# One range of 80 nodes per block, the edge attributes in the products, and gathers that no longer wait for the segment sums

## The reference

```python
f0 = x0 @ W1_0e / sqrt(32);  f1 = einsum('nui,uw->nwi', x1, W1_1o) / sqrt(32)
feat0, self0, feat1, self1 = halves of f0 and f1          # 32 units each
e0 = feat0[src];  e1 = feat1[src]                          # gather, 128 numbers per edge
ea0 = edge_attr_4[:, :1];  ea1 = edge_attr_4[:, 1:4]
h = gelu(gelu(edge_attr_8 @ W_mlp1 / sqrt(8)) @ W_mlp2 / 8)
w00, w01, w10, w11 = h @ Wp_..                             # 32 weights each, per edge
out0_a = w00 * e0 * ea0;              out0_b = w11 * sum(e1 * ea1) / sqrt(3)
out1_a = (w01 * e0) * ea1;            out1_b = w10 * e1 * ea0
n0, n1 = segment_sum of [out0_a, out0_b], [out1_a, out1_b] over dst
y = cos * self + sin * (n @ W2)                            # W2_0e, W2_1o
out = layernorm(x + y)
```

## Time and profile before

| | |
|---|---|
| median of the runs | 5078.59 us |
| the profiled execution | 5022.96 us, its span 5021.2 us |
| share of the span busy | PE 73%, PE weight loads 52%, DVE 37%, ACT 27%, POOL 63% |
| granted TensorE clock, mean | 0.861 |
| gathers | 3224 indirect DMAs, 211.52 MB, 16.2% of the 16 DMA engines |
| moved by DMA, mean | 51 GB/s |

### The profile page before, as it was taken

The page is one execution under the profiler, slowest core; times in us unless marked ns, Lnnn a source line. Parts: engine busy times, 40 slices in busy tenths (PEclk is TensorE's granted clock), DMA queues, the critical chain, the costliest instruction groups (busy, mean ns, idle before and its releaser), DMA issues.

```text
span 5021.2 us, 43952 instructions
## 1 busy us (share of the span) xinstructions
PE 3679.1 (73%) x13222; PEld 2590.0 (52%) x13222; DVE 1875.9 (37%) x4551; ACT 1335.7 (27%) x2651; POOL 3166.7 (63%) x3262
## 2 busy tenths in 40 slices
PE   7667777767777777767777777777777677777776
PEld 4445555545555555444555545554555455555555
DVE  4333333333333333333333334333433343334335
ACT  4222222222222222222222222222222222222224
POOL 5656666666666666666666666666666666666660
PEclk8888888888888888888888888898888888888887
DMA  4111111211111121111112111111111111111111
GB/s 162 48 43 48 50 46 48 50 47 47 49 49 48 46 50 48 47 47 46 45 47 50 48 46 50 48 48 49 47 48 50 46 48 50 48 47 47 48 45 57
DMA packets 244371, 254.65 MB, mean 51 GB/s; under 512 B 162332, under 2 KB 188703, under 8 KB 242800
## 3 DMA queue, kind: packets, MB, share of 16 engines
q0 software_dynamic: 103616, 211.52, 16.2%
q1 hardware_dynamic: 139024, 42.54, 3.4%
q10 hardware_dynamic: 1696, 0.18, 0.0%
HBM read 241.18 MB, written 12.80 MB: 51 GB/s over the span
## 4 chain that ended last, share of the span: by engine, by line
another core or an unknown queue 56%; PE 29%; ACT 8%; issue 6%; DVE 1%; ACTq 0%; DMA 0%; DVEq 0%; POOL 0%; POOLq 0%
PE bank L778 9%; PE bank L769 8%; PE bank L764 6%; ACT h L551 3%; PE bank L790 2%; PE bank L798 1%; ACT big L557 1%; ACT idx L536 1%; ACT ztsb L570 1%; ACT dst_rows L566 1%; ACT big L622 1%; ACT dst_rows L565 1%; ACT dst_rows L564 1%; PE bank L723 0%
## 5 line engine op out<-in xcount | busy, mean ns | idle before, releaser
L456 POOL DMA_INDIRECT gath<-feature_table,idx x3224 | 3144.5, 975 | 1733.1 <-issue 1598.8
L769 PE MATMUL bank<-h,w2bd 128*128 128x512 f32 x800 | 580.3, 816 | 1207.2 <-ACT h L551 1150.3
L1042 DVE TENSOR_TENSOR big<-bank,gath 128x256 f32<-128x256 f32 x606 | 254.3, 420 | 2947.8 <-remote 2807.5
L551 ACT ACTIVATE h<-bank 128x512 f32<-128x512 f32 x400 | 238.9, 597 | 3305.3 <-remote 2832.0
L790 PE MATMUL bank<-big,sel 128*128 128x256 f32 x4848 | 1081.3, 379 | 7.3 <-DVE big L1045 7.3
L778 PEld LDWEIGHTS bank<-wpbd,big 128*128 128x128 f32 x3224 | 742.4, 230 | 525.8 <-issue 358.3
L790 PEld LDWEIGHTS bank<-big,sel 128*128 128x128 f32 x4848 | 922.5, 190 | 133.3 <-issue 7.5
L778 PE MATMUL bank<-wpbd,big 128*128 128x256 f32 x3224 | 969.5, 441 | 1.2 <-DVE big L1045 1.2
L769 PEld LDWEIGHTS bank<-h,w2bd 128*128 128x128 f32 x800 | 151.6, 237 | 1379.9 <-ACT h L551 1316.7
L1045 DVE TENSOR_TENSOR big<-bank,gath 128x384 f32<-128x384 f32 x1212 | 613.5, 548 | 0.0
L1032 DVE TENSOR_TENSOR sel<-big,ea_t 128x512 f32<-128x512 bf16 x808 | 527.7, 694 | 0.0
(11 more groups left out here) (90 smaller groups left out, 1431.5 us busy)
## 6 DMA issues: line engine op xcount, KB each, us to landing
gath<-feature_table,idx POOLq DMA_INDIRECT x3224
e<-in_edge_attr SPq DMA_DIRECT2D x204, 64.0 KB
ea_t<-in_edge_attr SPq DMA_DIRECT2D x100, 64.0 KB
feature_table<-gath SPq DMA_DIRECT2D x4, 1280.0 KB, 6.8
out<-big SPq DMA_DIRECT2D x4, 1280.0 KB
big<-in_x SPq DMA_DIRECT2D x3, 1280.0 KB, 10.9
dst_rows<-in_dst SPq DMA_DIRECT2D x1, 1536.0 KB
big<-in_src SPq DMA_DIRECT2D x1, 1280.0 KB
```

Source lines behind the costliest of these rows:

```text
L456: pool.indirect_dma_start(out=gath[:, s % SLOTS, t, :], out_offset=None, in_=table[:, :], in_offset=bass.IndirectOffsetOnAxis(ap=idx[:, s, ...
L551: act.activation(h1[:, h, :], hid_ps[:, :], ACT.Gelu_apprx_tanh, scale=1.0 / math.sqrt(RADIAL)).then_inc(s_h1[h], 1)
L769: pe.matmul(hid_ps[:, :], w2bd[:, :], h1[:, h, :], start=True, stop=True).then_inc(s_h2p[h], 1)
L1042: dve.tensor_tensor(o[:, :, :, 0, :], w[:, :, :, 0, :], f[:, :, 0, :].unsqueeze(2).to_broadcast([128, n, 2, MUL]), ALU.mult)
```

## The change

The four attributes leave the selection and go into the products; a block has one range of 80 nodes instead of four of 32; chunks become two halves of eight tiles; indices, destinations and attributes come by DMA in the order in which they are used, four blocks at a time; and POOL waits only for the products that free a slot. The cores of the diff:

```diff
-CHUNKS = 4
-WINDOW = 32
+HALVES = 2
+HT = TILES // HALVES
+WINDOW = 80
...
 # SP: one DMA each for four blocks, in the place of ACT's casts and the prologue's transposes
+            def load_edges(half, start):
+                load_numbers(idx, src, half, start, s_idx[half])
+                load_numbers(dst_t, dst, half, start, s_dst_t[half])
+                load_attributes(half, start)
...
+                def reload_edges(half, n):
+                    sp.wait_ge(s_prod[1], n * RING + (SUPER * (half + 1) - RING))
+                    load_edges(half, n * (RING * BLOCK) + SUPER * half * BLOCK)
...
 # POOL
-                def gather_block(b, s, free, b_stop, chunks=range(CHUNKS), stops={}):
-                    pool.wait_ge(s_idx, b + 1)
-                    if b_stop is not None:
-                        pool.wait_ge(s_seg[CHUNKS - 1], b_stop)
-                        pool.sem_inc(s_round, 1)
-                    for c in chunks:
-                        if free is not None and c % 2 == 0:
-                            pool.wait_ge(s_prod[c + 1], free)
-                            pool.sem_inc(s_round, 1)
...
+                def gather_block(b, s, indices, free=None, tiles=TILES, stops={}):
+                    if indices is not None:
+                        pool.wait_ge(*indices)
+                        pool.sem_inc(s_round, 1)
+                    for h in range(-(-tiles // HT)):
+                        if free is not None:
+                            pool.wait_ge(s_prod[h], free)
+                            pool.sem_inc(s_round, 1)
...
+                        gather(s, range(HT * h, min(HT * (h + 1), tiles)))
...
 # ACT
-                act.copy(to[0:32], z_ps[pair][0:32, :, 0:128])
-                act.copy(to[32:64], z_ps[pair][32:64, :, 128:256])
-                act.copy(to[64:128], z_ps[pair][64:128, :, 128:256]).then_inc(s_zc, 1)
+                act.copy(zsb[0:WINDOW, :, :], z_ps[0:WINDOW, :].rearrange("w (k f) -> w k f", k=2)).then_inc(s_zc, 1)
...
 # PE
+            def segment_sum(b, s, tiles=TILES):
                 if s > 0:
+                    pe.wait_ge(s_zt, b)
+                for t in range(tiles):
+                    if t % HT == 0:
+                        pe.wait_ge(s_prod[t // HT], b + 1)
+                    last = pe.matmul(z_ps[0:WINDOW, :], sel[:, s % 2, t, :], mid[s % 2][:, t, :],
+                                     start=(t == 0), stop=(t == tiles - 1))
+                last.then_inc(s_seg, 1)
...
+                for k in range(2):
+                    last = pe.matmul(y_ps[:, 0:WINDOW * n], conv[:, k, :],
+                                     ztsb[:, k, 0:n, :].rearrange("q b w -> q (b w)"), start=(k == 0), stop=(k == 1))
...
 # DVE
+            def select(b, s, arrived, tiles=TILES):
...
+                    dve.wait_ge(s_seg, b - 1)
+                dve.scalar_tensor_tensor(sel[:, s % 2, 0:tiles, :],
+                                         dst_t[:, s % RING, 0:tiles].unsqueeze(2).to_broadcast([128, tiles, WINDOW]),
+                                         base_bc[:, bass.ds(b, 1)],
+                                         iota_ps.unsqueeze(1).to_broadcast([128, tiles, WINDOW]),
+                                         ALU.subtract, ALU.is_equal).then_inc(s_sel, 1)
...
+                dve.tensor_tensor(w[:, :, 0:2, :], w[:, :, 0:2, :], f[:, :, 0, :].unsqueeze(2).to_broadcast([128, n, 2, MUL]),
+                                  ALU.mult)
+                dve.tensor_tensor(w[:, :, 2, :], w[:, :, 2, :], scalar, ALU.mult).then_inc(s_scaled, 1)
+                dve.wait_ge(s_scaled, count * 2 + 1)
+                dve.tensor_tensor(o[:, :, 0, :], w[:, :, 0, :], scalar, ALU.mult)
+                dve.tensor_tensor(o[:, :, 1:4, :], w[:, :, 2, :].unsqueeze(2).to_broadcast(wide), f[:, :, 1:4, :], ALU.mult)
+                dve.tensor_tensor(o[:, :, 5:8, :], w[:, :, 1, :].unsqueeze(2).to_broadcast(wide), vector, ALU.mult)\
+                    .then_inc(s_scaled, 1)
+                dve.wait_ge(s_scaled, count * 2 + 2)
+                dve.tensor_tensor(w[:, :, 0:3, :], w[:, :, 3, :].unsqueeze(2).to_broadcast(wide), vector, ALU.mult)\
+                    .then_inc(s_dot, 1)
+                dve.wait_ge(s_dot, count + 1)
+                dve.tensor_tensor(w[:, :, 0:3, :], w[:, :, 0:3, :], f[:, :, 1:4, :], ALU.mult).then_inc(s_dots, 1)
+                dve.wait_ge(s_dots, count + 1)
+                return dve.tensor_reduce(o[:, :, 4, :], w[:, :, 0:3, :].rearrange("q t i u -> q t u i"), AXIS_X, ALU.add)
...
             def cycle(b, s, n, at=0):
                 if s >= 0:
+                    products(b, s, 1, n * 2 + s // SLOTS, ea_t[:, s % RING])
+                if s > 1 and s % CONV == 1:
+                    add_windows(b - 5, n * (RING // CONV) + s // CONV)
                 if s >= -1:
...
+                    select(b + 1, s + 1, arrived, LAST_TILES if last else TILES)
+                    attributes_arrived(b + 1, s + 1, n, at + 1)
+                    products(b + 1, s + 1, 0, n * 2 + (s + 1) // SLOTS, ea_short if last else ea_t[:, (s + 1) % RING],
```

More of the change, by code:

```diff
@@ L53 @@
 ROUNDS = (BLOCKS - 2) // RING
[L54 removed]
+assert BLOCKS == 2 + RING * ROUNDS and LAST_TILES <= HT
 MIX = math.pi / 8.0
@@ L795, in transpose_sums @@
-            def transpose_sums(b, first=0):
-                pe.wait_ge(s_zc, b * 2 + (2 - first // 2))
-                for c in range(first, CHUNKS):
-                    last = pe.transpose(zt_ps[:, 128 * c:128 * (c + 1)], zsb[:, c, :], ident[:, :])
+                if s > 0 and c % 2 == 0:
+                    pe.wait_ge(s_prod[c // 2], b)
+                for r in range(2):
+                    last = pe.matmul(wgt_ps[:, 512 * c + 256 * r:512 * c + 256 * (r + 1)],
+                                     h2[:, s // SUPER % 2, s % SUPER, 2 * c + r, :], wpbd[:, :], start=True, stop=True)
@@ L799, in transpose_sums, with convolve @@
+            def transpose_sums(b):
+                pe.wait_ge(s_zc, b + 1)
+                for k in range(2):
+                    last = pe.transpose(zt_ps[:, k, :], zsb[0:WINDOW, k, :], ident[0:WINDOW, 0:WINDOW])
                 last.then_inc(s_ztp, 1)
-            def convolve(b, n=CONV):
+            def convolve(b, after, n=CONV):
                 pe.wait_ge(s_zt, b + n)
-                pe.wait_ge(s_add[CHUNKS - 1], b + 1)
-                for k in range(4):
-                    last = pe.matmul(y_ps[:, 0:128 * n], conv[:, k, :],
-                                     ztsb[:, k, 0:n, :, :].rearrange("q b c w -> q (b c w)"), start=(k == 0), stop=(k == 3))
+                pe.wait_ge(s_sel, after)
+                for k in range(2):
+                    last = pe.matmul(y_ps[:, 0:WINDOW * n], conv[:, k, :],
+                                     ztsb[:, k, 0:n, :].rearrange("q b w -> q (b w)"), start=(k == 0), stop=(k == 1))
@@ L1062, in load_bases @@
-                    min_val=0, max_val=NODES - 1,
-                    skip_runtime_bounds_check_because="a destination is a node's number by the kernel's contract")
-                return base
-            def add_windows(b, s, done, base, first=0):
+                    base_row[0:1, bass.ds(b, n)], engines=(mybir.EngineType.DVE,),
+                    min_val=0, max_val=NODES - WINDOW,
+                    skip_runtime_bounds_check_because="a base is at most the last window's by the prologue's minimum")
@@ L1067, in add_windows @@
+                return base
+            def add_windows(b, done, n=CONV):
+                base = load_bases(b, n)
                 dve.wait_ge(s_y, done)
-                for c in range(first, CHUNKS):
-                    dve.wait_ge(s_add[c - 1 if c > first else CHUNKS - 1], b + 1)
-                    at = bass.ds(base[c], WINDOW)
-                    y_at = WINDOW * (CHUNKS * (s % CONV) + c)
-                    dve.tensor_tensor(acc[:, at], acc[:, at], y_ps[:, y_at:y_at + WINDOW], ALU.add).then_inc(s_add[c], 1)
```

691 lines of the change are left out of this document (278 added, 413 removed).

## The result

The changed kernel takes 5596.15 us (median of four, 5570.55 to 5611.78) and the kernel before 5189.99 us (four runs, 5057.23 to 5417.26). The kernel before has faster executions (5057.23, 5078.59) and slower ones (5301.39, 5417.26) at a lower granted clock, for which no trace here gives a reason; ratios in this document compare the faster ones alone. The ratio is 1.104, 95% interval 1.095 to 1.113: the changed kernel is 10% slower. The profiled execution of the changed kernel took 5608.05 us (span 5606.2), 585 us more than that of before, where the prediction had 357 us more (5380).

A forecast was written before the change was run, and what follows sets the result against it. POOL's gathers, plus a gap per block that lets PE's held signals out, bound the kernel. 5023 + 394 (longer blocks) - 28 (old long bursts) - 25 (prologue) + 15 (tail) = 5380 us; range 4600 to 5700, the forecast's own 5150 to 5700.

The forecast's parts named there:

- The bound and the mechanism: POOL's gap per block lets out PE's signals, held during gather bursts; without it blocks go from 23.9 to 25.9 us; chance 0.47.
- The signs named for the forecast: Bursts of 24 or 32 gathers, then 8 us or more idle; PE idle 10 us; DVE's remote waits ahead of the comparison.
- DVE: DVE's work goes from 9.3 to 14.6 us a block; half the products 6.4 us, with the comparison 7.8 us.
- PE's round: PE's own chain for a block, from 2407.55 to 2424.0 plus 0.7 us for the gelu: 17.2 us.
- POOL's 1.24 us gathers: One gather per block slowed beside DVE's selection, 1.24 instead of 0.95 us; the 0.3 us may go.
- The period of 25.9 us: Block time in the steady loop: 51.8 us for two blocks, 25.9 each instead of 23.9, adding 394 us over 197 blocks.
- The steps up to 16.4 us: From a first half's end: second half at 6.4 us, segment sums 8.6, comparison and products 16.4, before gathers end at 20.2.
- POOL runs until no slot is free: Late in the burst: 32 gathers, 41.1 us, then 2.85 us for signals and 7.8 us for a half slot: 51.8 us.
- The upper bounds, 26.7 and more: Block period bounds from measured long bursts: 26.7 us (12.25 us idle) to 30.4 us (19.6 us idle).
- POOL's start at 55.25 stays within some us: Prologue: POOL's first gather stays near 55.25 us, since the table is stored only then.
- Tail: Three to four blocks without gathers at the end, each 4 to 5 us longer by DVE's chain: +15 us.
- The gather floor: Rival in the steady loop: PE's signals prompt, POOL never stops, bound by gathers, 4260 us; chance 0.18.

The follow-up runs named there:

- e1: Changed kernel with POOL's stop for the segment sums put back ahead of each block: 5025.22 us, ratio 0.992 to the kernel before.
- e2: Kernel before with only POOL's stop for the segment sums taken away: median 5623.06 us (5486.25 to 5637.09).
- e6: Changed kernel, POOL waiting after each block's 16 gathers until they have landed, then on a short scratch fill: 5068.19 us.
- e7: Changed kernel without stop, POOL waiting for a scratch fill of 1280 columns after every 8 gathers: 4935.82 us.
- e12: Kernel before, its stop replaced by two waited-for fills of 16 columns after every 8 gathers: 5112.99 us.
- e3: Changed kernel with every second gather left out from the fifth block on, old rows used instead: 3786.23 us.
- e18: Changed kernel with the 73-row destination load cut in two, neither stop nor pause: 4149.43 us against 4216.89 before, ratio 0.984.
- e8: Changed kernel without stop, a small scratch fill of 128 columns after every single gather: 6656.76 us.
- e10: Changed kernel without stop, 73-row load cut in two, a waited-for fill of 512 columns after every 8 gathers: 5290.8 us.
- e9: Changed kernel without stop, 73-row load cut in two, a waited-for fill of 16 columns after every 8 gathers: 5731.66 us.
- e4: Changed kernel, POOL waiting after each block's 16 gathers until the last has landed, without a fill: 5708.2 us.
- e5: Changed kernel with POOL's stop put back and the 73-row destination load cut into 64 and 9 rows: 4956.12 us.

## Why the prediction was right in sign and wrong in size

**The bound and the mechanism: right.** POOL's gap for the stop was what let PE's signals out. It is worth 10% of the changed kernel (e1) and 8% of the one before (e2); a gap without it does its work (e6, e7, and most of it in e12). The signs named for the forecast came in part: bursts of 24 or 32, each followed by 8 us of idle, with PE idle for 10 us within them. They are of 24 and 8, POOL waits a median of 4.7 us after 24 and 10.5 us after 8, and PE is idle for 8.05 us. DVE's "remote" waits are more at the first product (L935, 837.6 us) than at the comparison (L920, 389.3 us), which is the other way round than forecast.

**DVE: right.** 14.1 us a block for 14.6; a half of the products 6.1 to 6.2 for 6.4; comparison and half 7.7 for 7.8. **PE's round: right** while signals are prompt; the chain without held signals is 17.8 us (e3), 17.2 in the working. **SP: right**; no wait for indices stands among POOL's waits. **POOL's 1.24 us gathers: right, and small.** The mean gather went from 975 to 946 ns, 0.46 us a block; I had named it and taken nothing. The new comparison reads PSUM on one side. By the Trainium skill (SBUF — State Buffer, "Who interferes with whom") a DVE instruction with at most one input in SBUF, outside the 2-port modes, doesn't contend with GpSimd: the trace agrees (every gather from 2436 to 2494 us takes 0.94 or 0.95 us).

**The period of 25.9 us: the term that was mis-sized.** The last gather of the changed kernel:

```profile
5475.40 0.95 POOL L424 DMA_INDIRECT gath<-feature_table,idx  x1 [0.30 <-issue]
```

First gather to end of the last is 5476.4 - 82.5 = 5393.9 us, where before's 4912.7 - 55.3 is 4857.4: +537, for which the sum had 394 - 28 - 25 = +341. This is 196 of the 228 us that were missing. The steps up to 16.4 us held, as these rows of the changed kernel show:

```profile
2437.03 0.96 DVE L949 TENSOR_REDUCE big<-weights 128x256 f32<-128x768 f32 x1
...
2439.88 7.07 PE L710 MATMUL bank<-dst_rows,sel 128*80 128x256 f32 x32
...
2443.15 0.96 DVE L949 TENSOR_REDUCE big<-weights 128x256 f32<-128x768 f32 x1
...
2454.07 0.96 DVE L949 TENSOR_REDUCE dst_rows<-weights 128x256 f32<-128x768 f32 x1
...
2471.12 0.29 ACT L523 COPY ztsb<-bank 128x160 f32<-128x160 f32 x1 [12.70 <-remote]
```

From the end of a first half at 2437.99 (t = 0) the second half is done at 6.1 us (6.4 in the working) and the next block's first half at 17.0 (16.4), and POOL has met no gap. The step that failed is the next one, "POOL runs until no slot is free: 32 gathers, 41.1 us; then 2.85 us until the signals are out and 7.8 us until a half slot is free". It lets POOL use a fourth half that isn't done: that half waits for weights behind a held signal (DVE idle for 11.20 us until 2466.22), so POOL runs dry after 24 gathers. And it has the next segment sums finished, with only their signal held, when POOL runs dry. In the trace they haven't begun, because ACT's copy of the sums before them waits for PE's signal too (12.70 us). They start at 2471.47, 3.0 us after the last gather, and take 9.55 us, where the working had 6.9 and the same sums take 7.07 us at 2439.88; the granted clock is 0.74 from 2471.4 to 2481.1, after PE's 8.05 us of idle, and 1.00 from 2439 to 2447. POOL restarts at 2473.21 on the late half, the next one isn't free, and 8 gathers (10 us) must cover sums, comparison and products (19.8 us from 2471.47 to 2491.24). So there are two dry spells per two blocks, 4.73 + 9.10 = 13.8 us for 10.65; over the kernel 6.8 us of waits a block for 5.3, less 0.5 us of shorter gathers. The upper bounds, 26.7 and more, held the truth (26.8); I took the worked value, though the long burst that I had measured said 26.7.

**"POOL's start at 55.25 stays within some us": wrong,** by 27 us. I had counted what the change took from the prologue and not its new loads: 73 rows of 8 KB on a queue's way. 20 of the 27 come back with the load in two. **Tail: +21 for +15.** The changed kernel's tail is 129.9 us after the last gather, before's 108.5. 196 + 27 + 6 are the 228 us, within 1.

**The gather floor, a rival with 0.18,** is what the other condition gives. I worked it out at 4260 us; the changed kernel with the load in two takes 4149. The parts are 61 us to the first gather (55 in the working), 4023 us of gathers (4062) and a tail of 63 us (124): where POOL is the bound, few blocks are left when it ends. The kernel before takes 4215 there; no trace of that execution is on record. The Trainium skill's rule (TensorE: Matmul & The Clock Gate, "The cost: per-tile semaphore tail", a signal some tens of ns after the matmul's end) fits that condition, where the recorded moments in e18 are 0.01 us after the modelled end, and fails in the one that was timed, where PE's consumers started 7 us late. The single trace that I had could not tell that both exist.

**Not settled:** which resource holds the signals back, what switches the condition, whether bytes or numbers of gathers count (the two runs that asked met the other condition), and where between 1.39 and 1.49 us the limit lies. Where signals are held back, the kernel with the stop and the load in two (4956.12 us) and the one with pauses of 1280 columns (4935.82) were faster than the kernel before beside them (5326.92, one run of each); against its shortest executions on other chips (5029 to 5098) they are 1.5 to 3% ahead. Where signals are prompt, the pauses cost 13 to 15%. The stop should cost nothing there, since the kernel before has it and takes 4215 us, but the changed kernel with the stop was not run there.

## What to carry to other kernels

An idle gap on the engine that issues gathers can be what lets other engines' signals through. Before a wait in front of gathers is removed as useless, look at what resumes at its end, and at what a burst without the gap looks like where the trace happens to have one; price the change by that burst and not by a sum of parts. And where one kernel is found in two conditions (here 5030 to 5420 us and 4215 us), time a change in both: this one loses 10% in the first and gains 1.6%, with the load in two, in the second. A wait that ends when the work is done (the stop) looks safer than a fixed pause, which costs 13 to 15% where nothing is held back.

## What the hardware showed unasked

- PE's signals under gathers from POOL: prompt at a mean spacing of 1.49 us (e7) and 1.96 us (e8), late at 1.39 us and below (e10, e9), in one condition; never late in the other, at 1.25 us (e18). The signals of ACT, DVE and POOL are late in neither.
- Traces of the first condition lack a part of the semaphores' recorded increments (PE's: 1406 of 1623 are there in the changed kernel), traces of the second have them all.
- A gap of 2.59 us after 16 gathers (e4) doesn't clear the backlog, 3.5 us (e6, second half of the kernel) does, and 2.06 us after each 8 (e7) does.
- A DMA of 73 rows of 8 KB ran at some 27 GB/s for its last 12 us and more, with the DMA engines' share under a tenth; as 64 and 9 rows it did not show (e5).
- A fill on POOL that POOL waits for costs 0.8 to 0.9 us more than its own length before the next gather starts.
